# Gathers as one stream into two buffers, the x0b transfers put one by one over the block, and the multilayer weights laid out contiguously on chip

## What is computed

```python
e = jnp.stack([tbl_0[ids[:, 0]], ..., tbl_31[ids[:, 31]]], axis=1)      # 1024 x 32 x 16
x0 = e; xk = x0; outs = []
for W in (W0, W1, W2):                                                  # 32 x 32 x 64, 32 x 64 x 64 twice
    xk = relu(einsum('bmd,bhd,mhk->bkd', x0, xk, W))
    outs.append(sum(xk, axis=2))
z = concatenate(outs, axis=1)
h = concatenate([z, dense_ctx], axis=1)                                 # 1024 x 208
h = maximum(h @ W_top1 + b_top1, 0.0)                                   # 512 columns
h = maximum(h @ W_top2 + b_top2, 0.0)                                   # 256 columns
y = h @ W_top3
```

## Time and profile before

| | |
|---|---|
| median of 3 runs | 791.03 us (784.43 to 791.82) |
| the profiled execution | 797.63 us, its span 795.8 us |
| TensorE matmul (PE) busy | 656.4 us, 82% |
| VectorE (DVE) busy | 551.6 us, 69% |
| GpSimd (POOL) busy | 464.6 us, 58% |
| ScalarE (ACT) busy | 310.7 us, 39% |
| granted TensorE clock, mean | 0.953 |
| DMA | 121.57 MB, mean 153 GB/s |

### The profile page before, as it was taken

One profiled execution on the slowest core, in us unless ns is written; L12 is line 12 of the kernel. 1 busy time (PEld: TensorE's weight loads), 2 busy tenths in 40 slices (PEclk: granted clock), 3 DMA queues, 4 the chain that ended last, 5 costly groups with the idle time before them and its releaser, 6 DMA issues.

```text
span 795.8 us, 8373 instructions
## 1 busy us (share of the span) xinstructions
PE 656.4 (82%) x3096; PEld 268.9 (34%) x3096; DVE 551.6 (69%) x274; ACT 310.7 (39%) x586; POOL 464.6 (58%) x332
## 2 busy tenths in 40 slices
PE   0047798797989789897999799996988879999987
PEld 0012133233443334333443244433432334434435
DVE  1005796976939496796859496794939679798581
ACT  0004261616334171624535271714517072717131
POOL 6756687673838667358838667383956733335100
PEclk9999999898989899998999999899999999999998
DMA  7569749691983739663698749473793919872000
GB/s 182 125 185 229 207 137 212 177 208 37 259 237 72 147 116 224 183 144 75 183 205 212 141 139 229 156 160 58 212 229 100 199 46 255 216 168 45 0 1 0
DMA packets 59112, 121.57 MB, mean 153 GB/s; under 512 B 15369, under 2 KB 32017, under 8 KB 58977
## 3 DMA queue, kind: packets, MB, share of 16 engines
q1 hardware_dynamic: 40336, 112.41, 57.3%
q10 hardware_dynamic: 10544, 6.53, 2.8%
q0 software_dynamic: 8192, 2.11, 2.8%
HBM read 116.82 MB, written 5.25 MB: 153 GB/s over the span
## 4 chain that ended last, share of the span: by engine, by line
PE 47%; issue 15%; DVE 10%; ACT 9%; another core or an unknown queue 9%; POOL 9%; DMA 1%; DVEq 0%; ACTq 0%; POOLq 0%
PE acc L632 38%; DVE z_dve L373 9%; POOL emb L320 8%; ACT xq L449 4%; PE psm L701 3%; ACT xq L441 3%; PE psm L710 2%; PE acc L647 2%; ACT xs L441 1%; DMA emb<-in_tbl_dram,ids_cur 1%; PE psm L688 1%; POOL z_pool L329 1%; PE psm L678 1%; DVE zacc L398 0%
## 5 line engine op out<-in xcount | busy, mean ns | idle before, releaser
L373 DVE TENSOR_TENSOR z_dve<-xq,x0b 128x2048 f32<-128x2048 f32 x210 | 464.6, 2285 | 128.5 <-ACT xq L441 99.5
L632 PE MATMUL acc<-z_dve,w_cin 128*64 128x512 f32 x1680 | 393.5, 603 | 29.6 <-DVE z_dve L373 19.9
L329 POOL TENSOR_TENSOR z_pool<-x0b,xs 128x2048 f32<-128x2048 f32 x46 | 208.4, 4560 | 165.3 <-ACT xs L441 163.7
L320 POOL DMA_INDIRECT emb<-in_tbl_dram,ids_cur x256 | 246.7, 964 | 83.7 <-issue 80.2
L632 PEld LDWEIGHTS acc<-z_dve,w_cin 128*64 128x64 f32 x1680 | 119.6, 138 | 277.1 <-issue 206.4
L441 ACT ACTIVATE xq<-acc 64x512 f32<-64x512 f32 x128 | 73.0, 570 | 268.8 <-remote 151.7
L449 ACT ACTIVATE xq<-acc 32x512 f32<-32x512 f32 x256 | 144.4, 564 | 24.9 <-DVE z_dve L373 15.5
L373 DVE TENSOR_TENSOR z_dve<-xq,x_rot 128x2048 f32<-128x2048 f32 x30 | 68.0, 2292 | 41.1 <-PE acc L632 24.7
L632 PE MATMUL acc<-z_dve,w_sym 128*64 128x512 f32 x256 | 71.3, 639 | 19.0 <-issue 11.4
L632 PE MATMUL acc<-z_pool,w_cin 128*64 128x512 f32 x368 | 85.9, 602 | 0.0
L647 PE MATMUL acc<-z_extra,w_extra 128*64 128x128 f32 x256 | 31.0, 319 | 27.9 <-issue 25.7
(11 more groups left out here) (39 smaller groups left out, 188.6 us busy)
## 6 DMA issues: line engine op xcount, KB each, us to landing
x0b<-x0t SPq DMA_DIRECT2D x120, 512.0 KB
x_rot<-x0t SPq DMA_DIRECT2D x64, 512.0 KB
x_rep<-x0t SPq DMA_DIRECT2D x16, 512.0 KB
emb<-in_tbl_dram,ids_cur POOLq DMA_INDIRECT x256
x0b<-x0t SPq DMA_DIRECT2D x16, 256.0 KB
x0t<-emb_t ACTq DMA_DIRECT2D x14, 256.0 KB, 2.6
w_cin<-in_L_rec_W_dram SPq DMA_DIRECT2D x16, 64.0 KB
x_lo<-x0t SPq DMA_DIRECT2D x16, 64.0 KB
```

The lines of the kernel that those rows point to most:

```text
L320: nc.gpsimd.indirect_dma_start(out=emb[:, D * f:D * f + D], out_offset=None, in_=tables[f], in_offset=bass.IndirectOffsetOnAxis(ap=ids_cur ...
L329: nc.gpsimd.tensor_tensor(z_pool[:, k % ZP_SLOTS, :, :], x0b[b % 2][:, 2 * j:2 * j + 2, :], xs[:, :].unsqueeze(1).broadcast_to([P, 2, N]), ...
L373: nc.vector.tensor_tensor(z_dve[:, k % Z_SLOTS, :, :], in0.unsqueeze(1).broadcast_to([P, 2, N]), in1, ALU.mult).then_inc(z_made, 1)
L632: ins = nc.tensor.matmul(acc[l][K * side:K * side + K, :], weights[c], z[:, c, NH * side:NH * side + NH], start=start and c == 0, stop=sto ...
```

## The change

1. `pick_ids` and `ids_cur` are gone: a gather takes its ids from `ids_all`. `emb` is two buffers, tile t in `emb[t % 2]`, with a semaphore for each. The gathers of tiles 1 to 7 are one stream of 224: 16, then `extra(0)`, then 6, then 20 for every block, 10 before and 10 after `extra(b+1)`, until the stream is used up (in block 10). The first gather of a tile t > 1 waits for the transposes of tile t-2.
2. Of `x0b(b+1)`, the first half's four transfers are gated one by one on the first four of VectorE's products of layer 1 of block b. The second half comes after `load_l0(b+2)`, its four transfers gated on the first four products of layer 2 of block b. Those gates take the place of the wait for the end of layer 2 of block b-1.
3. The weights `W_top1` and `W_top2` are loaded into slots 1 and 2 of `z_pool`, and ACT copies them in three instructions, after the first piece of tile 0, into an order that `mlp1` and `mlp2` read contiguously. POOL and TensorE wait once for these copies.

```diff
+GATHER_FIRST, GATHER_BLOCK = 22, 20
...
-        ids_cur = sb("ids_cur", [P, M], I32)
-        emb = sb("emb", [P, M * D])
+        emb = [sb(f"emb{i}", [P, M * D]) for i in range(2)]
...
+            def load_x0b(b, c0, z_gates):
+
                 for r in range(4):
-                    sp.dma_start(x0b[b % 2][Q * r:Q * r + Q, c0:c1, :],
-                                 x0_rows(b, r + 4 * c0, [[0, Q], [4 * ROW, c1 - c0], [1, N]])
+                    sp.wait_ge(z_made, z_gates[r])
+                    sp.dma_start(x0b[b % 2][Q * r:Q * r + Q, c0:c0 + CH // 2, :],
+                                 x0_rows(b, r + 4 * c0, [[0, Q], [4 * ROW, CH // 2], [1, N]])
                                  ).then_inc(x0b_in[b % 2][c0 // (CH // 2)], 16)
...
-                    load_x0b(b + 1, 0, CH // 2)
-                    load_x0b(b + 1, CH // 2, CH)
+                    load_x0b(b + 1, 0, [z_before[1, b, v, j] + 1 for v, j in l1_dve(b)[:4]])
...
                     load_l0(b + 2)
+                if b < LAST:
+                    load_x0b(b + 1, CH // 2, [z_before[2, b, NAT, j] + 1 for j in range(PAIRS)])
...
+            def gather_later(i0, i1):
+                for i in range(i0, min(i1, (TILES - 1) * M)):
+                    t, f = 1 + i // M, i % M
+                    if f == 0 and t > 1:
+                        pool.wait_ge(emb_transposed, GRP * (t - 1))
+                    gather(t, f, gathered[t % 2])
...
-            pick_ids(0)
-            for g in range(GRP):
-                gather(M // GRP * g, M // GRP * (g + 1), gathered0[g])
-            pool.wait_ge(emb_transposed, GRP)
-            pick_ids(1)
-            gather(0, 12)
+            for f in range(M):
+                gather(0, f, gathered0[f // (M // GRP)])
+            gather_later(0, GATHER_FIRST - 6)
             extra(0)
-            gather(12, 18)
+            gather_later(GATHER_FIRST - 6, GATHER_FIRST)
+            pool.wait_ge(w_summed, 2)
+            pool.wait_ge(mlp_ordered, 3)
             for b in range(BLOCKS):
                 pool.wait_ge(xs_ready, b + 1)
-                pool.wait_ge(w_summed, 2)
                 for j in pool_pairs(b):
                     multiply(b, j)
...
+                g = GATHER_FIRST + GATHER_BLOCK * b
+                gather_later(g, g + GATHER_BLOCK // 2)
                 if b < LAST:
                     extra(b + 1)
-                if tile < TILES:
-                    gather(mid, end)
+                gather_later(g + GATHER_BLOCK // 2, g + GATHER_BLOCK)
...
-            move_first_tile()
+            move_first_tile(0, 1)
             act.wait_ge(mlp_in, 6 * 16)
+            for i in range(2):
+                nc.scalar.copy(wt1_s[i][:, :, :],
+                               wt1_in[i].rearrange("p (f c) -> p c f", c=JC1)).then_inc(mlp_ordered, 1)
+            nc.scalar.copy(wt2_s[:, :, :, :],
+                           wt2_in.rearrange("p c (f j) -> p c j f", j=JC2)).then_inc(mlp_ordered, 1)
+            move_first_tile(1, GRP)
...
-                        ins = nc.tensor.matmul(psm[:, P * jc:P * jc + P], wt1_s[i][:, jc:F1:JC1], zsum[i][:, :],
+                        ins = nc.tensor.matmul(psm[:, P * jc:P * jc + P], wt1_s[i][:, jc, :], zsum[i][:, :],
...
-                        ins = nc.tensor.matmul(psm[:, P * jc:P * jc + P], wt2_s[:, c, jc:F2:JC2],
+                        ins = nc.tensor.matmul(psm[:, P * jc:P * jc + P], wt2_s[:, c, jc, :],
```

## The result

The kernel after takes 917.87 us (median of four runs, 915.83 to 923.12) against 791.42 for the kernel before beside it: a ratio of 1.160, 95% interval 1.154 to 1.166. I had forecast 861 us, at most 905. Its profiled execution took 916.28 us, with a span of 914.5 and a mean granted clock of 0.884 (before: 0.953).

A forecast was written before the change was run, and what follows sets the result against it. POOL's trip with its gathers, which starve TensorE, was taken as the bound. Intervals 1 to 9 +79.2, 10 to 14 -8.4, start +2.1 - 0.5, end -1.9 took 797.6 to 868.1, as a median 861 us; range 800 to 905.

The forecast's parts named there:

- What bounds the kernel before: 12 intervals of about 46 us bound by POOL's trip with its gathers, two of 36 to 40 by TensorE.
- Runs full for some 18 us: TensorE in back-to-back gathers: full for some 18 us, then instructions come only singly until the gathers end.
- The longer stretch: Gather stretch per block grows from 20.1 to 25.1 us; interval between 44.0 and 50.9 us, 49 taken in even blocks.
- The two gates: Tiles 6 and 7 wait for transposes in blocks 6 and 8, making those intervals 51.8 and 52 us.
- Rival C: Gathers starve TensorE but the second half of x0b is in time: median 819 us, chance 0.07.
- The late half: Second half of x0b lands late in odd blocks; POOL's third product waits 15.8 us, odd intervals take 59.7 us.
- TensorE's 7.7 us: Layer 1 of odd blocks: TensorE gets POOL's third product 7.7 us late, at 315.6 instead of 307.92.
- The start: Before block 1: ids copy gone, -0.5 us; block 0's 20 gathers end at 109.0, so multiply(1) starts 2.1 us later.
- The weights: Contiguous weight loads gain 1.6 us in mlp1 and 0.3 in mlp2; 1.6 in blocks 11 and 13, 1.9 at the end.
- A: Bursts of transfers, not gathers, starve TensorE, and spread out they no longer do: median 807 us, chance 0.13.
- B: A, and the late half is not so late, a wait of 9.2 us: median 762 us, chance 0.07.
- D: Nothing of ACT's work gets through in longer stretches: odd intervals 66.7, even 50.9; median 900 us, chance 0.12.

The follow-up runs named there:

- The two runs above: Kernel before, changed two ways: gathers of tiles 2 to 7 replaced by small POOL products, 711.3 us; x0b transfers from block 3 on cut to 16 columns, 803.3 us.
- 12 and 14: Longest gather pieces: 2, 2, 12 on the kernel before, weights ordered, third product later, 747.2 us; 3, 3, 14 on the kernel after, half early, 766.2 us.
- e4: Kernel after with the second half of x0b issued ahead of the x0t wait and load_l0, still one by one behind gates: 823.0 us.
- e5: Kernel after with POOL's wait for tile 0's transposes put back before the first gather of tile 1: 919.8 us.
- e3_weights: Kernel before with only the weights of the multilayer part put in order on chip: 788.0 us, ratio not resolved.
- e7_small_x0b: Kernel before with x0b transfers of blocks 3 and up moving 16 of 512 columns, gathers kept: 803.3 us.

## Why the prediction was wrong, step by step

- **What bounds the kernel before: right.** POOL's trip with its gathers and a TensorE starved by them. The two runs above separate this from the bursts and from POOL's load; without most of its gathers, and so without starving, the kernel before takes 711 us.
- **"Runs full for some 18 us": wrong.** It held for the earlier trace rows because those stretches have nearly the same work in them. The quantity is some 120 to 170 of TensorE's instructions. For the forecast it did not matter, since after's stretches are all longer; it would have cost me any forecast of shorter pieces, as with 12 and 14.
- **The longer stretch: right.** In the run without the late half intervals 3, 4 and 5 are 51.7, 51.4 and 51.9, where 50.9 was the upper bound. 49 in even blocks came out as 44.7 and 51.4. The two gates (51.8 and 52) measured 52.3 and 52.1. Rival C, gathers starve and the half in time, is that run: 819 forecast, 823.0 measured. Within it, though, a start 17 too short stood against blocks 1 to 9 eleven too long and an end five too long.
- **The late half: the step that failed, by size.** The place, the blocks, the releaser and the 7 us that `x2_nat` and `x2_swp` win back are as forecast (block 5: 19.7 waited, 12.2 lost against e4). Two sizes were off. First the landing: I took bytes and the mean rates of the earlier trace rows, 274 and 201 GB/s, and got 19.8 us from the issue of `x_rep`; in block 5 it took 23.7, and 22.1 to 26.6 over the seven odd blocks. Of this, 0.7 us was arithmetic: `load_l0` is 2.75 MB and not 2.69, so 4.85 MB were due, and I took 311.1 where my own sum gave 311.5. These rates give 20.5 us. The rest is the rate, 4.85 MB at 205 GB/s: a window's rate counts bytes of transfers that have not landed, and a transfer lands with its slowest part. So POOL's waits in blocks 1 to 9 were 85 us in sum and not 61, which is 24 of the 26 us missing there. Second, blocks 11 and 13, which have no gathers: I gave them TensorE's 7.7 us and 1 for the clock; against 38.0 in e4 they lost 14.0 and 14.4. In block 11 TensorE waits 12.10 us for the third product, and the pair behind the wait takes 1.75 us longer, 3.64 us at a granted clock of 0.5 against 1.89 at 1.0 in e4. That is 13.9 of the 14.0:

```profile
705.88 3.64 PE L645 MATMUL acc<-z_pool,w_cin 128*64 128x512 f32 x8 [12.10 <-POOL z_pool L344]
```

  The wait in block 5 comes apart in the same way. TensorE waited 13.39 us there and not 7.7, because the product was 3.9 us later than forecast and TensorE, with a shorter `mlp1` ahead, was there 1.8 us earlier. In all I priced the half at 42 us (861 against rival C's 819); it is 95.
- **The start: wrong.** The step was "they end at 109.0, so `multiply(1)` starts at 109.0". It left out what I had put into every other trip, that a starved TensorE and `xs` follow the gathers by 6 us (5.98 us idle before 125.60). The row, in the kernel after:

```profile
125.60 4.55 POOL L344 TENSOR_TENSOR z_pool<-x0b,xs 128x2048 f32<-128x2048 f32 x1 [5.98 <-ACT xs L448]
```

  And I looked for the effect of 48 gathers in a row on POOL alone, not on TensorE's warm-up, which starves in them: 6.5 us by e5. The other 4 stay in e5, which like after has four more gathers ahead of the loop than before; that they are the cause is not tested. That makes the first product 10.6 us later and block 0 35.8 us long instead of 27.7, in all 18.7 us where I had 1.6.
- **The weights: right in direction, too small.** `mlp1`'s matmuls went from 397 to 275 ns, 16 x 0.122 = 2.0 us for a tile where I had taken 1.6, and two tiles lie in the end (6 and 7) where I counted one. The loads of both lines, after (min/median/max ns):

```profile
L714 PEld LDWEIGHTS psm<-zsum,wt x64: 186/190/192, 248.4 to 907.3; 128*128 128x128 f32 x64
L723 PEld LDWEIGHTS psm<-h,wt_s x128: 186/192/334, 285.4 to 910.9; 128*128 128x128 f32 x128
```

  `mlp2`'s had a median of 196 ns before, with a step of two floats, and has 192 now: the step was free. The 215 of the earlier trace rows was a mean with loads at the lower clock in it. The Trainium skill (SBUF — State Buffer, the note on cachelines under Door 1), by which two hits in a 16-byte line are enough, is borne out, and I was wrong to set it aside for that row. The two `mlp1` together give 4.1 of the 7.2 us. The rest is the clock: in before the last `mlp2` takes 3.74 us and not 2.02, and the two pairs behind tile 6's `mlp1` 5.00 and not 3.65. Windows around the two `mlp1` of the end, of before, then of e3_weights (granted clock third from the end; the stretches don't hold equally many matmuls):

```profile
733.00:745.00 12.00, 11.48 (x44) 5.75 (x42) 12.00 (x7) 4.02 (x9) 5.93 (x2) 0.86 0.00 1
780.00:796.00 16.00, 10.34 (x60) 9.29 (x60) 0.69 (x1) 2.44 (x9) 0.00 (x0) 0.78 0.00 0
```

```profile
727.00:738.00 11.00, 10.48 (x56) 4.46 (x56) 11.00 (x6) 4.02 (x9) 5.51 (x2) 1.00 0.00 1
773.00:782.20 9.20, 4.70 (x37) 4.00 (x36) 0.00 (x0) 2.44 (x9) 0.00 (x0) 1.00 0.00 0
```

  All ten kernels with ordered weights have an end of 63.3 us, the seven without 68.6 to 70.5. That the order keeps the clock up is a reading of these rows; how is open.
- **The rivals.** A and B fall with the bursts. D, nothing of ACT's work gets through, came true in block 4 alone (51.4), not in odd blocks. The range left out what happened because its upper end (D) varied how much of ACT's work gets through, and not how late the half is, though both ends of its rate were there to take: 201 GB/s throughout gives 4.85 / 0.201 = 24.1 us, where 23.7 was measured.

## What to carry to other kernels

Before a transfer is moved down a queue, ask which wait it now stands behind and who uses it first; then time its landing by the lowest rate that such a stretch shows, because a mean over a window counts bytes of transfers that are not in yet. Where an engine is starved by a neighbour, look for the quantity that is constant over the stretches (here the instructions, not the time), because it says how short a piece must be, and look at the stretches that fall out of line: here they point to a short pause as a remedy that is still to be tried. Work that must be done in any case is better cut up and placed between other pieces of its engine than gathered at the end: the same 16 gathers a block as 4, 4 and 8 with the products between them, the third product used later and the weights in order, make the kernel 10% faster instead of 16% slower.

## What the runs showed of the hardware that I had not expected

- While GpSimd issues indirect DMAs back to back, TensorE gets through some 120 to 170 instructions and then one or two every 1.4 us, also with hardly a transfer under way (DMA share 0.07 in e7_small_x0b). Small products on GpSimd of nearly the same total time do not do it. One product of 4.6 us between gathers is enough to start the count again. `extra`, with 0.65 us between its two gathers, is not, but in four stretches in which it came later, with 1.3 to 1.9 us between them, TensorE got through some 175 to 243.
- The Trainium skill (Runtime: NRT & Kernel Launch, Instruction fetch mechanics) has an engine fetch blocks of instructions over its own DMA queue. In the kernel before one packet of the queue "q8 instruction" went through in the stretch of gathers from 300.24 to 320.4 us, and TensorE starved at its end all the same. So in this trace it is not such a fetch that was held up; the mechanism behind the count stays open.
- Of transfers of 0.52 MB queued behind each other, in the kernel after, one landed every 2.4 to 3.1 us (the half of block 5: 372.9, 375.3, 377.8, 380.9 us).
